# Two stages joined with the layer norm behind them, in a hybrid block on one Trainium2 core

## The reference

```python
x = x + neural_memory(layernorm(x), ...)   # one gradient step on W0, W1; then read
x = x + product_keys(layernorm(x), ...)    # 8 heads, 64 x 64 keys, top 8; experts
x = x + attention(layernorm(x), ...)       # 16 heads of 16, causal
x = x + product_keys(layernorm(x), ...)

def neural_memory(x, ...):                 # the end of it, the memory read
    return silu((x @ Wq.T) @ W0n.T) @ W1n.T @ Wout.T

def attention(x, ...):                     # the end of it, the attention output
    return softmax(...) @ V @ W_o

def product_keys(inputs, gamma, beta, ...):
    mu, var = mean(inputs, axis=0), var(inputs, axis=0)   # of each feature over all rows
    xn = (inputs - mu) * rsqrt(var + eps) * gamma + beta
    ...
```

## Time and profile before

| | us |
|---|---|
| median of 3 runs (lowest, highest) | 3638.61 (3636.14, 3642.56) |
| the profiled execution | 3640.09 |
| its span | 3638.3 |
| TensorE, VectorE, ScalarE, GpSimd busy | 3213.3, 2964.9, 1570.6, 676.2 |
| mean granted clock of TensorE | 0.949 of full |

### The profile page before, as it was taken

The page is one execution under the profiler, slowest core; times in us unless marked ns, Lnnn a source line. Parts: engine busy times, 40 slices in busy tenths (PEclk is TensorE's granted clock), DMA queues, the critical chain, the costliest instruction groups (busy, mean ns, idle before and its releaser), DMA issues. The chain is left out here.

```text
span 3638.3 us, 75919 instructions
## 1 busy us (share of the span) xinstructions
PE 3213.3 (88%) x29442; PEld 2250.7 (62%) x29442; DVE 2964.9 (81%) x8984; ACT 1570.6 (43%) x2146; POOL 676.2 (19%) x353
## 2 busy tenths in 40 slices
PE   3997579999999986789999999997379999999997
PEld 2886357778787875533333333334257787878786
DVE  5443799999999995788888888871599999999996
ACT  1221244444444441635666666664244444444441
POOL 0000023333333332010000000000023333333333
PEclk6999699999999998979999999998699999999999
DMA  5534600000000001851221212004600000000000
GB/s 180 194 101 142 206 7 10 19 10 19 10 19 10 19 8 42 228 90 27 44 48 32 38 29 47 7 6 116 233 10 10 14 16 16 13 19 10 19 7 16
DMA packets 203794, 190.52 MB, mean 52 GB/s; under 512 B 49910, under 2 KB 182326, under 8 KB 203062
## 3 DMA queue, kind: packets, MB, share of 16 engines
q1 hardware_dynamic: 201526, 184.22, 18.5%
q10 hardware_dynamic: 1920, 1.57, 0.2%
HBM read 121.05 MB, written 64.29 MB: 51 GB/s over the span
## 5 line engine op out<-in xcount | busy, mean ns | idle before, releaser
L521 PE MATMUL f_p_route<-f_x_w,f_y_hot 128*128 128x64 f16 x8192 | 897.3, 193 | 87.3 <-DVE f_weighted L793 76.0
L545 PE MATMUL f_p_out<-f_kout,f_hidden 128*128 128x256 f16 x6144 | 853.4, 273 | 17.9 <-POOL f_hidden L450 16.7
L534 PE MATMUL f_p_hid<-f_xtc,f_kin_t 128*128 128x256 f16 x6144 | 852.9, 273 | 4.8 <-ACT f_hidden L633 4.7
L450 POOL TENSOR_TENSOR f_hidden<-f_weighted,f_hidden 128x1024 f16<-128x1024 f32 x256 | 612.1, 2391 | 1278.1 <-DVE f_x_w L783 1273.7
L1999 DVE TENSOR_REDUCE at_part_max<-at_p_ring 128x1 f32<-128x512 f32 (+3 forms) x1280 | 706.2, 603 | 119.5 <-PE at_p_ring L1870 75.1
L521 PEld LDWEIGHTS f_p_route<-f_x_w,f_y_hot 128*128 128x128 f16 x8192 | 691.3, 98 | 136.4 <-issue 111.1
L545 PEld LDWEIGHTS f_p_out<-f_kout,f_hidden 128*128 128x128 f16 x6144 | 601.5, 98 | 196.8 <-issue 118.6
L1980 ACT ACTIVATE at_prob<-at_p_s 128x1024 f32<-128x1024 f32 (+3 forms) x640 | 546.5, 895 | 382.2 <-PE at_p_s L1916 190.7
L534 PEld LDWEIGHTS f_p_hid<-f_xtc,f_kin_t 128*128 128x128 f16 x6144 | 601.4, 98 | 77.9 <-issue 10.2
L638 ACT CAST f_hidden<-f_weighted 128x1024 f16<-128x1024 f32 x256 | 343.3, 1341 | 580.7 <-DVE f_weighted L793 580.7
L633 ACT ACTIVATE f_hidden<-f_p_hid 128x512 f32<-128x512 f32 x512 | 301.5, 595 | 438.5 <-PE f_p_hid L534 437.8
(11 more groups left out here) (252 smaller groups left out, 3190.2 us busy)
## 6 DMA issues: line engine op xcount, KB each, us to landing
at_q<-qk SPq DMA_DIRECT2D x42, 256.0 KB, 4.6
at_k<-qk SPq DMA_DIRECT2D x42, 256.0 KB, 4.4
f_ln_xin<-x SPq DMA_DIRECT2D x16, 512.0 KB, 6.3
xt<-f_ln_xt SPq DMA_DIRECT2D x32, 256.0 KB, 6.0
f_kin_t<-kin_t SPq DMA_DIRECT2D x8, 1024.0 KB, 8.5
f_xt_in<-xt SPq DMA_DIRECT2D x32, 256.0 KB, 2.9
f_kout<-kout_parts SPq DMA_DIRECT2D x8, 1024.0 KB, 8.1
f_xres<-x SPq DMA_DIRECT2D x32, 256.0 KB, 2.7
```

The source lines that it names most:

```text
L450: nc.gpsimd.tensor_tensor(lo, weighted[s % WR], hi, ALU.subtract).then_inc(lo_ready, 1)
L521: last = nc.tensor.matmul(p_route[:, t, :], y_hot[:, s % HR, t // PAIR, :, t % PAIR], x_w[:, s % HR, half, t // PAIR, :, t % PAIR], start= ...
L534: last = nc.tensor.matmul(p_hid[g % 2][:, xp % 2, :], kin_t[:, a, dh, xp * P:(xp + 1) * P], xt[slot][:, b, dh, :], start=i % 6 == 0, stop= ...
L545: last = nc.tensor.matmul(p_out[:, u, :], parts[slot][:, xp, u * P:(u + 1) * P, a], kout[:, b, xp, :], start=g == 0 and i == 0, stop=xp == ...
```

## The change

The layer norm is no stage of its own in the experts' steps. A class `FeatureNorm` holds its buffers and gives each engine one step to do behind each chunk of another stage. The memory read and the attention output get this class and run in one block with it: they write their residual rows into `FeatureNorm.y` in SBUF (three blocks of 512 rows), from where the statistics and the normalisation read them; the rows are still stored to HBM for the residual that follows. The steps of a block are spread over later chunks (`LEAD`). Loops become straight-line code. The memory read moves from the memory's step to the experts' step, so the barrier and clearing of semaphores that lay behind it now lie in front of it, and `first_w`, `second_w` outlive their step. It reads its transposed rows from `xt0`, apart from the `xt` that the norm writes. The loads of `kin_t`, `kout` and `wct` are put at given chunks (`KIN_AT`, `KOUT_AT`). Attention stores its rows as 4096 x 256, so that a chunk of them is loaded in one piece. The memory's own first layer norm keeps the old function.

```diff
+NY = 3
+KIN_AT, KOUT_AT = (1, 5, 9, 13), (15, 17, 18, 19)
...
+class FeatureNorm:
+    LEAD = 5
...
+        self.y = [sb(f"y{i}", [P, BT, D]) for i in range(NY)]
+        self.xln, self.xt = ([sb(f"{n}{u}", [P, BT, D]) for u in range(2)] for n in ("xln", "xt"))
+        self.xt = [x[:].rearrange("p t d -> p (t d)").rearrange("p (h b) -> p h b", h=DH) for x in self.xt]
+        self.stats, self.mv = ([sb(f"{n}{u}", [P, BT, w]) for u in range(2)] for n, w in (("stats", 6), ("mv", 2)))
...
+    def rows_of(self, c):
+        return self.y[c // 2 % NY][:, c % 2 * 2:c % 2 * 2 + 2, :]
+    def wait_rows_free(self, dve, c):
+        m = c // 2
+        if c % 2 == 0 and m >= NY:
+            dve.wait_ge(self.y_stored[m % NY], ONE + m // NY * 32)
+            dve.wait_ge(self.xln_ready, ONE + m - NY + 1)
+    def store_rows(self, sp, c, y_rows):
+        sp.wait_ge(self.y_ready, ONE + c + 1)
+        sp.dma_start(y_rows[:, c * 2:c * 2 + 2, :], self.rows_of(c)).then_inc(self.y_stored[c // 2 % NY], 16)
+    def statistics(self, dve, chain, m):
+        nc, u = self.nc, m % 2
+        dve.wait_ge(self.y_ready, ONE + 2 * m + 2)
+        if m >= 2:
+            dve.wait_ge(self.xln_ready, ONE + m - 1)
+        for t in range(BT):
+            chain.mark(nc.vector.bn_stats(self.stats[u][:, t, :], self.y[m % NY][:, t, :]))
+        chain.wait()
+        nc.vector.memset(self.gate[:], 0.0)
+        for t in range(BT):
+            chain.mark(nc.vector.bn_aggr(self.mv[u][:, t, :], self.stats[u][:, t, :]))
+        chain.wait()
+        nc.vector.tensor_scalar_add(self.var_eps[u][:], self.mv[u][:, :, 1], LN_EPS).then_inc(self.var_ready, 1)
+    def normalise(self, dve, chain, m):
+        nc, u = self.nc, m % 2
+        dve.wait_ge(self.root_ready, ONE + m + 1)
+        chain.link(newton_reciprocal(nc, chain, self.rstd[u][:], self.rstd[u][:], self.var_eps[u][:], self.tmp))
+        if m >= 2:
+            dve.wait_ge(self.xt_ready, ONE + m - 1)
+        for t in range(BT):
+            last = nc.vector.tensor_scalar(self.xln[u][:, t, :], self.y[m % NY][:, t, :], self.mv[u][:, t, 0:1],
+                                           self.rstd[u][:, t:t + 1], ALU.subtract, ALU.mult)
+        last.then_inc(self.xln_ready, 1)
+    def count(self, dve, m):
+        dve.wait_ge(self.xt_copied, ONE + m + 1)
+        for h in range(DH):
+            last = self.nc.vector.bn_stats(self.bn_st[:, h, m, :], self.xt[m % 2][:, h, :])
+        last.then_inc(self.counted, 1)
...
+    def vector_step(self, dve, chain, c):
+        if c % 2 == 0 and 0 <= c // 2 - 1 < NBLK:
+            self.normalise(dve, chain, c // 2 - 1)
+        if c % 2 and c // 2 < NBLK:
+            self.statistics(dve, chain, c // 2)
+        if c % 2 and 0 <= (c - 5) // 2 < NBLK:
+            self.count(dve, (c - 5) // 2)
+    def tensor_step(self, pe, c):
+        m = (c - 3) // 2
+        if c % 2 and 0 <= m < NBLK:
+            pe.wait_ge(self.xln_ready, ONE + m + 1)
+            if m >= 2:
+                pe.wait_ge(self.xt_copied, ONE + m - 1)
+            for t in range(BT):
+                for h in range(DH):
+                    last = self.nc.tensor.transpose(self.pxt[m % 2][:, h, t * P:(t + 1) * P],
+                                                    self.xln[m % 2][:, t, h * P:(h + 1) * P], self.ident[:])
+            last.then_inc(self.xt_ready, 1)
+    def scalar_step(self, act, c):
+        m = c // 2 - 1
+        if c % 2 == 0 and 0 <= m < NBLK:
+            act.wait_ge(self.var_ready, ONE + m + 1)
+            self.nc.scalar.activation(self.rstd[m % 2][:], self.var_eps[m % 2][:], ACT.Sqrt).then_inc(self.root_ready, 1)
+        m = c // 2 - 2
+        if c % 2 == 0 and 0 <= m < NBLK:
+            act.wait_ge(self.xt_ready, ONE + m + 1)
+            if m >= 2:
+                act.wait_ge(self.xt_stored[m % 2], ONE + m // 2 * 16 * (BLK // CH))
+                act.wait_ge(self.counted, ONE + m - 1)
+            self.nc.scalar.copy(self.xt[m % 2], self.pxt[m % 2][:]).then_inc(self.xt_copied, 1)
+    def sync_step(self, sp, c):
+        m = (c - 5) // 2
+        if c % 2 and 0 <= m < NBLK:
+            sp.wait_ge(self.xt_copied, ONE + m + 1)
+            for k in range(BLK // CH):
+                sp.dma_start(self.xt_dram[m * (BLK // CH) + k, :, :, :],
+                             self.xt[m % 2][:, :, k * CH:(k + 1) * CH]).then_inc(self.xt_stored[m % 2], 16)
+        self.load_ahead(sp, c)
+    def wait_stored(self, sp):
+        for u in range(2):
+            sp.wait_ge(self.xt_stored[u], ONE + 16 * NBLK // 2 * (BLK // CH))
+        for i in range(NY):
+            sp.wait_ge(self.y_stored[i], ONE + 32 * len(range(i, NBLK, NY)))
...
+            def load_ahead(sp, c):
+                if c == 1:
+                    with nc.allow_non_contiguous_dma(reason="512 scalars"):
+                        sp.dma_start(gb[:, 0, :], gamma.rearrange("(h p) -> p h", p=P)).then_inc(gb_loaded, 16)
+                        sp.dma_start(gb[:, 1, :], beta.rearrange("(h p) -> p h", p=P)).then_inc(gb_loaded, 16)
+                if c in KIN_AT:
+                    i = KIN_AT.index(c)
+                    k = slice(i * NE // 4, (i + 1) * NE // 4)
+                    sp.dma_start(kin_t[:, :, :, k].rearrange("p a h e -> p (a h) e"),
+                                 kin_dram[:, :, :, k].rearrange("p a h e -> p (a h) e")).then_inc(weights_loaded, 16)
+                if c == KIN_AT[-1]:
+                    sp.dma_start(wct[:], wct_dram).then_inc(weights_loaded, 16)
+                    sp.wait_ge(norm.xt_stored[0], ONE + 16 * (BLK // CH))
+                    sp.dma_start(xt_in[:], xt_dram[0, :, :, :]).then_inc(xt_loaded, 16)
+                if c in KOUT_AT:
+                    i = KOUT_AT.index(c)
+                    k = slice(i * NX // 4, (i + 1) * NX // 4)
+                    sp.dma_start(kout[:, :, k, :].rearrange("p a x d -> p a (x d)"),
+                                 kout_dram[:, :, k, :].rearrange("p a x d -> p a (x d)")).then_inc(kout_loaded, 16)
...
@@ memory_read, sync @@
-            def next_xt(u, i):
-                sp.wait_ge(pre_ready[u], ONE + i + 1)
-                load_xt(u, i + 1)
-            def finish(u, i, last=False):
-                sp.wait_ge(y_ready[u], ONE + i + 1)
-                if not last:
-                    load_x(u, i + 1)
-                sp.dma_start(out_rows[:, bass.ds((i * 2 + u) * 2, 2), :], y[u][:]).then_inc(y_stored[u], 16)
-            for u in range(2):
-                load_xt(u, 0)
-                load_x(u, 0)
-            next_xt(0, 0)
-            with sp.Fori(0, n_it - 2) as i:
-                next_xt(1, i)
-                finish(0, i)
-                next_xt(0, i + 1)
-                finish(1, i)
...
+            def load_xt(c):
+                above(sp, pre_ready, c - 1)
+                sp.dma_start(xt[c % 2][:], xt_dram[c, :, :, :]).then_inc(xt_loaded[c % 2], 16)
+            def load_x(c):
+                above(sp, norm.y_ready, c - 1)
+                sp.dma_start(x[c % 2][:], rows[:, c * 2:c * 2 + 2, :]).then_inc(x_loaded[c % 2], 16)
+            load_xt(0)
+            load_xt(1)
+            load_x(0)
+            load_x(1)
+            norm.load_ident(sp)
+            for c in range(NCH + norm.LEAD - 1):
+                if c + 2 < NCH:
+                    load_xt(c + 2)
+                if c < NCH:
+                    if c + 2 < NCH:
+                        load_x(c + 2)
+                    norm.store_rows(sp, c, out_rows)
+                norm.sync_step(sp, c)
+            norm.wait_stored(sp)
...
@@ memory_read, tensor, scalar, vector @@
+            pre(0)
+            norm.wait_ident(pe)
+            for c in range(NCH + norm.LEAD - 1):
+                if c + 1 < NCH:
+                    pre(c + 1)
+                if c < NCH:
+                    out(c)
+                norm.tensor_step(pe, c)
...
+            sigmoid(0)
+            for c in range(NCH + norm.LEAD - 1):
+                if c + 1 < NCH:
+                    sigmoid(c + 1)
+                norm.scalar_step(act, c)
+            norm.feature_root(act)
...
+            chain = Chain(dve, norm.steps)
+            hidden(0)
+            for c in range(NCH + norm.LEAD - 1):
+                if c + 1 < NCH:
+                    hidden(c + 1)
+                if c < NCH:
+                    residual(c)
+                norm.vector_step(dve, chain, c)
+            norm.feature_scales(dve)
...
@@ attention_units @@
-                sp.dma_start(ao_dram[n, qb * BLK:(qb + 1) * BLK, :].rearrange("(t p) c -> p t c", p=P),
+                g = n % (NU // BATCH)
+                first = n // (NU // BATCH) * SEQ + qb * BLK
+                sp.dma_start(ao_dram[first:first + BLK, g * GD:(g + 1) * GD].rearrange("(t p) c -> p t c", p=P),
...
@@ attention_output @@
-            def load_rows(u, b, j):
-                for t in range(2):
```

(52 more changed lines are left out.)

315 lines of the change are left out of this document (109 added, 206 removed).

## The result

The changed kernel takes 3653.04 us (median of 6 runs, 3647.64 to 3657.55), the one before on the same chip 3640.47 (6 runs, 3636.14 to 3642.79): ratio 1.0034, interval 1.0021 to 1.0047. It is slower by 12.6 us, where 20.8 us less were forecast. One of the seven executions of e9 took 6390 us, and no trace shows why; its ratio leaves it out.

The account below looks back on a forecast made before the run. TensorE and VectorE took turns; once joined, SyncE's issue order would set the pace. Memory 121.3 against 124.9 us and attention 109.1 against 126.3 gave 20.8 us less: 3640.1 to 3619.3, median 3618 us, range 3606 to 3632.

Parts of the forecast that it names:

- The loop through SyncE's queue: Joined stages: residual, SyncE's issues, input landing, products, next residual set the pace; residuals 1 to 13 take 71.0 and 63.8 us.
- land: Joined loops: input lands 4.4 us after the residual, 5.9 with block stores, 9.0 with keys too, 8.0 after chunk 1.
- The reaction behind the landing: Joined loops: landing to residual's end takes 4.8 us in memory, 3.6 in attention, plus a cold-clock addition.
- The clock's share: Joined loops: TensorE's lower clock after waits adds 1.3 us six times in memory, 7.8 us; in attention 6.6 us.
- The ends: Last residual to routed experts, each joined stage: 14.6 us of transfers, 2.1 of start, 0.5 more, 17.2 us.
- The starts: Joined stages up to residual 1: memory 17.6 us; attention 14.5 us from the old first load.
- 13 to 15: Joined stages, residual 13 to 15: VectorE decides, 7.7 us in memory and 7.0 in attention.
- rivals 4: Joined stages: all inputs land as late as the layer norm's loads, 6.3 us; no change, 3638 us; chance 0.14.
- rival 5: Joined stages: each input lands like a 1 MB load, in 8.5 us; 47 us more, 3665 us; chance 0.13.
- Rival 1: Joined stages: large loads do not hold small ones up; 8.3 us less a part, 3601 us; chance 0.17.
- rival 3: Joined memory stage: ScalarE's activation table switches come into the loop without keys; 6 us, 3624 us; chance 0.08.
- rival 2: Joined stages: engines set the pace because inputs are always early, 58 and 48 us; 3556 us; chance 0.03.

Follow-up runs that it names:

- e9: Changed kernel with TensorE multiplying constants while it waits for inputs in the memory read: 3648.78 us, ratio 1.0027 to the kernel before.
- e1: Changed kernel with inputs issued one chunk earlier, ahead of SyncE's wait for the residual: 3605.22 us, ratio 0.9914 to the kernel before.
- e12: Changed kernel where SyncE still waits for the residual but issues the input first, ahead of stores and keys: 3608.88 us, ratio 0.9918 to the kernel before.
- e5: Changed kernel with inputs issued one chunk earlier, keys and wct on ScalarE's queue, values behind the last transposed stores: 3575.82 us, 0.9826 of the kernel before.
- e7: Changed kernel with four buffers for each input in place of two: 3573.8 us, ratio 0.9824 to the kernel before.
- e8: Changed kernel with four input buffers, keys and wct on ScalarE's queue, values behind the last transposed stores: 3556.69 us, ratio 0.9775 to the kernel before.
- e10: Changed kernel with the keys in sixteen 256 KB loads, one a chunk, instead of four of 1 MB: 3623.95 us, ratio 0.9963 to the kernel before.
- e15: Kernel before with only the attention rows stored as 4096 x 256, nothing joined: 3639.24 us, ratio 1.0001 to the kernel before.
- e13: Kernel before, unchanged, profiled once more: 3637.72 us (one run).
- e4: Kernel before with only the attention output joined to its layer norm, memory read as before: 3639.64 us, ratio 1.0004 to the kernel before.
- e2: Changed kernel with keys and wct issued by ScalarE's queue at the same chunks: 3621.29 us, ratio 0.9956 to the kernel before.
- e6: Changed kernel with the square root of each block replaced by a copy (output wrong): 3648.1 us, ratio 1.0028 to the kernel before.
- e11: e8 with the square root of each block replaced by a copy (output wrong): 3557.29 us, ratio 0.9776 to the kernel before.

## Why the prediction was wrong

**The mechanism was right.** The loop through SyncE's queue exists as forecast, with the waits where the forecast had them (TensorE for xt and rows) and the longest loops where the keys are loaded; two chunks take 9 to 18 us, forecast 8 to 14. And e1, e12, e5, e7 and e8 show that it is the price: with the input issued sooner the same 12 chunks of memory take 64.5, then 51 to 47 us, in place of 85.

**The terms that failed.** The chief one is "land": 1.9 us and a queue at 342 GB/s, from the residual to the landing 9.0 us with keys, 5.9 with the block's stores, 4.4 with nothing, 8.0 after chunk 1. Measured to the first product in memory, loop by loop: 10.2, 4.9, 11.8, 6.2, 11.5, 6.4 against 8.0, 4.4, 9.0, 5.9, 9.0, 5.9, 8.7 us more; in attention 10.6, 5.1, 11.5, 6.3, 11.2, 6.3, also 8.7 us more. Of these 17.4 us 14.7 lie in the six loops with keys. The issues were right (2.89 us where I had 3.0).

The step that failed is the price of the 1 MB of keys. The 9.0 us are 0.18 + 1.9 of start, 0.77 for each of x, y, the two stores and the input, and 3.07 for the keys, so every transfer up to the input was counted; but all went at 342 GB/s, a rate taken from the layer norm with its 512 KB and 1 MB loads. Measured, the keys land behind what was issued ahead of them by 4.3, 5.5 and 4.6 us in memory and 5.2, 4.7 and 4.5 in attention, 10.3 us more in six loads. What stands ahead of them landed 0.5 to 1.0 us later than that sum each time, 4.7 in all, and the input followed the keys by 0.6 to 0.7, where I had 0.77. From its own issue a load of keys took 7.4 to 8.9 us, as in the earlier trace rows, where it is 8.5; my queue gave it 5.9. So the row that had the right number was on the page, and I replaced it by a rate. In the kernel before, six of the eight same loads landed 2.5 to 3.0 us behind the store ahead of them, so 342 GB/s did hold there; in the loop shown above 221 GB/s were moved from 345.5 to 348 us, as the stores ended and the keys began, with the DMA engines at 0.95. No run shows why the rate is lower. That a large load in one place matters, and not the bytes in all, is confirmed by e10: the same bytes in smaller loads, one a chunk, are 16.9 us less in the two times 12 chunks.

The reaction behind the landing, with the cold clock, was 34.1 us in six loops in memory, forecast 36.6, and 29.8 in attention, forecast 28.2. The clock's share I had at 7.8; over the 4.45 us of a loop at the full clock (e9) the six in memory took 1.8, 0, 1.8, 1.7, 2.1 and 0, 7.4 in all.

**The ends**, forecast 17.2, were 21.3 and 22.7: 9.6 us more. In memory the last copy ended 10.8 us behind the residual, not 8.5, since it waited for a store that stood behind the keys and wct of chunk 13; I had let that backlog out. Behind it 10.5 us, not 8.7. My 14.6 us of transfers at 342 GB/s were 5.0 MB; from 407 to 428.5 us 373 GB/s were moved, 8.0 MB. The rate was better than mine, the bytes were not counted.

**The starts**: memory 1.0 us more, attention 2.4. The first load of the new attention stage comes 5.24 us behind the last attention store (2511.76 - 2506.52):

```profile
2506.52 0.36 SPq L1949 DMA_DIRECT2D attn_rows<-at_ao  x1
...
2511.76 0.37 SPq L2208 DMA_DIRECT2D ao_rows<-attn_rows  x1
```

The old first load came 2.46 us behind it, so the seam costs 2.8 us, as I took it for memory (3.1); I let it be given back in attention by loads in one piece, and it was not.

**What I compared with.** The first profile of before had a slow attention output, 128.6 us against 123.9 in the second. In e15, with the old output too, it was 126.5. So of the 17.2 us that attention's part seemed to have to give up to 4.7 were scatter of one profile.

**The sum.** To the forecast of 3619.3 us as an execution come loops 6.1 + 10.3, ends 9.6, starts 3.3, 13 to 15 -0.7, all else 6.4: 35 us, which is the profiled execution (3655.0) within 1 us. All else had been put at nothing (bounds 0 to 3): in e13, e15 and e4, with the old memory read, it was 3386.8 to 3389.4 us, so a good part of the 6.4 is the first profile's low 3384.8. Sign and size of the error are thus those terms, above all the landing. The result lies between the rivals 4 (3638) and 5 (3665): landings in the keys loops are 7.5 to 8.9 us, those of the others 3.2 to 4.2, on the mean 6.0, just under the 6.3 from which rival 5 was to decide. Rival 1, that large loads don't hold small ones up, is out by e2 and e10; rival 3 by e6 and e11; rival 2 was no forecast for this order, but the four buffers reach its pace.

## What to carry to other kernels

When two stages are laid over each other, list for each input what its queue issues between the event that frees its buffer and the load, in bytes. A fused stage can close loops that the separate ones didn't have, and here the saved engine time was worth nothing until the inputs were issued a full landing ahead. Price a landing by everything that the queue still holds, and take for a large load ahead of it the time that the profile lists for that load, not its bytes at the rate of the best stream. A deeper buffer (here 8 KB per partition) cured this without moving any load, and moving the bulk loads to another queue than the transfers that somebody waits for took 29.6 us off the two parts.

## What the runs showed of the hardware that was not expected

- In the loop around a 1 MB load, 4.3 to 5.5 us lie between the landing of what was issued ahead of it and its own; in the layer norm of the kernel before it was 2.5 to 3.0 in six of eight.
- Of one queue, part of the transfers issued behind a 256 KB load were through before it had landed: 3.0 MB moved, 2.36 issued up to it.
- The DMA engines at 0.95 to 1.01 busy moved 221 to 323 GB/s in the loops (loads and stores of 256 KB among one of 1 MB), and 373 and 356 at 0.99 and 0.97 in the ends. A busy share alone is no rate.
- The granted clock fell to 0.50 within a wait of 8 us of TensorE, and the first product behind it took 3.78 us instead of 1.89. Constant matmuls in the wait kept it at 1.00.
